# One expert tile fewer, and the last two shared tiles finished one by one on VectorE

## The reference

```
scores = softmax(xf @ gate_w.T)
weights, idx = top_k(scores, 2)
eo   = (silu(xf @ w1[e].T) * (xf @ w3[e].T)) @ w2[e].T      # for each expert e
y    = sum over the two chosen experts of weight * eo
z    = silu(xf @ ws1.T) * (xf @ ws3.T) @ ws2.T              # the shared expert
x    = layernorm(x + y + z)                                  # the block's output
```

## Time and profile before

| | |
|---|---|
| time, median of 3 runs | 1658.03 us (1657.46 to 1659.5) |
| time of the profiled execution | 1656.27 us |
| span of the profiled execution | 1654.5 us |
| PE busy | 1608.0 us, 97% of the span |
| DVE, ACT, POOL busy | 820.9, 654.7, 706.5 us |
| granted TensorE clock, mean | 0.99 |

### The profile page before, as it was taken

The page is one execution under the profiler, slowest core; times in us unless marked ns, Lnnn a source line. Parts: engine busy times, 40 slices in busy tenths (PEclk is TensorE's granted clock), DMA queues, the critical chain, the costliest instruction groups (busy, mean ns, idle before and its releaser), DMA issues.

```text
span 1654.5 us, 31031 instructions
## 1 busy us (share of the span) xinstructions
PE 1608.0 (97%) x9466; PEld 1352.2 (82%) x9467; DVE 820.9 (50%) x2239; ACT 654.7 (40%) x1564; POOL 706.5 (43%) x774
## 2 busy tenths in 40 slices
PE   7999999999999999999999999897999999999997
PEld 6898999899999989998999899875677777777764
DVE  5555556655655656566556655565222222222365
ACT  4444334433443344334334433443233333333455
POOL 3323333333343243333432433433555555555465
PEclk9899999999999999999999999999999999999999
DMA  8112111110111020111111201348355555556686
GB/s 287 35 62 60 33 33 52 44 32 32 52 43 32 32 63 32 32 32 63 32 32 32 63 32 32 115 139 270 87 102 103 102 102 103 102 104 126 198 302 234
DMA packets 83916, 143.19 MB, mean 87 GB/s; under 512 B 10664, under 2 KB 27560, under 8 KB 83328
## 3 DMA queue, kind: packets, MB, share of 16 engines
q1 hardware_dynamic: 59792, 95.96, 17.6%
q0 software_dynamic: 18304, 38.24, 13.2%
q10 hardware_dynamic: 5776, 8.43, 1.9%
HBM read 94.75 MB, written 56.76 MB: 92 GB/s over the span
## 4 chain that ended last, share of the span: by engine, by line
PE 92%; DMA 3%; DVE 2%; issue 1%; POOL 1%; ACT 1%; SPq 0%; ACTq 0%; POOLq 0%; DVEq 0%
PE bank L1151 32%; PE bank L1076 16%; PE bank L1245 11%; PE bank L1103 10%; PE bank L1226 7%; PE bank L1200 6%; PE bank L1184 3%; PE bank L1213 3%; PE bank L1050 3%; DMA bx<-x_d 1%; PE bank L1086 1%; DMA passing<-in_wqkvT 1%; DMA bx<-x_d,idxc 0%; DVE zs L1740 0%; POOL w13l L719 0%
## 5 line engine op out<-in xcount | busy, mean ns | idle before, releaser
L1151 PE MATMUL bank<-wh,xh 128*128 128x512 f32 (+2 forms) x896 | 338.8, 378 | 2.8 <-DVE wl L1355 2.8
L1151 PE MATMUL bank<-wl,xh 128*128 128x512 f32 (+2 forms) x896 | 327.5, 365 | 0.0
L1151 PE MATMUL bank<-wh,xl 128*128 128x512 f32 (+2 forms) x896 | 326.7, 365 | 0.0
L668 POOL TENSOR_TENSOR rnorm<-ssmax,nhalf 128x4 f32<-128x4 f32 x128 | 131.8, 1030 | 389.8 <-DVE ssmax L1391 384.6
L1151 PEld LDWEIGHTS bank<-wh,xh 128*128 128x128 f32 x896 | 170.1, 190 | 29.7 <-DVE wl L1355 2.2
L1151 PEld LDWEIGHTS bank<-wh,xl 128*128 128x128 f32 x896 | 169.8, 190 | 28.4
L1151 PEld LDWEIGHTS bank<-wl,xh 128*128 128x128 f32 x896 | 170.3, 190 | 22.5
L1377 DVE TENSOR_TENSOR bl<-bank,bh 128x512 fp32r<-128x512 f32 x104 | 71.6, 689 | 179.0 <-ACT bh L830 178.9
L756 POOL DMA_INDIRECT eo_d<-eo,dstc x72 | 115.3, 1602 | 101.4 <-ACT eo L1015 76.4
L1245 PE MATMUL bank<-woh,oh 128*128 128x256 f32 (+1 forms) x512 | 147.5, 288 | 0.9 <-DVE xr L1461 0.9
L1245 PE MATMUL bank<-wol,oh 128*128 128x256 f32 (+1 forms) x512 | 144.8, 283 | 0.0
(11 more groups left out here) (201 smaller groups left out, 3490.4 us busy)
## 6 DMA issues: line engine op xcount, KB each, us to landing
eo_d<-zero_d SPq DMA_DIRECT2D x34, 256.0 KB, 3.0
xt<-in_xT SPq DMA_DIRECT2D x33, 256.0 KB, 3.2
xr<-in_x SPq DMA_DIRECT2D x32, 256.0 KB, 2.7
x_d<-xr SPq DMA_DIRECT2D x32, 256.0 KB, 2.1
eo_d<-xr SPq DMA_DIRECT2D x32, 256.0 KB, 2.3
bx<-x_d SPq DMA_DIRECT2D x32, 256.0 KB, 5.7
ga<-eo_d SPq DMA_DIRECT2D x16, 512.0 KB, 5.4
gb<-eo_d SPq DMA_DIRECT2D x16, 512.0 KB, 6.9
```

Source lines behind the costliest of these rows:

```text
L668: pool.tensor_tensor(rnorm[:, :], ssmax[:, :], nhalf[:, :], ALU.pow).then_inc(rn_s, 1)
L1151: mm = pe.matmul(b[:, 0:n], a[:, par, c, :], wt[:, c, cols], start=(c == 0 and k == 0), stop=(c == DC - 1 and k == 2))
```

## The change

Three things change. First, `NX` stays 71. A few constants follow: the pattern of `jp128` is still made for an even count (`NXP` = 72), the two semaphores that count the scatters of even and odd tiles wait for 36 and 35 of them, and the written-out tail of `tile_steps` starts at step 76 in place of 80, so the hardware loop has 15 iterations in place of 16 and three more expert tiles are written out behind it.

Second, for the last pair the product of each tile is not copied into `zs` by ACT. DVE's new `finish_tile` adds the bank and `ga` of one tile (128x512) into `zs`, takes its statistics, adds eps, waits for POOL's one power instruction (`tile_power`), and subtracts the mean and multiplies with a `tensor_scalar` into `oo`. It does this for tile 30, then for tile 31. Third, SP's last two stores wait for DVE's new semaphore `last_s`.

```diff
-NX += NX % 2
+NXP = NX + -NX % 4
...
-            for q in range(S1 + NX - 4, NQ + 1):
+            for q in range(4 * ((S1 + NX - 4) // 4), NQ + 1):
...
-                    sp.wait_ge(o_s, 2 * n + k + 1)
+                    sp.wait_ge(*((last_s, k + 1) if n == LAST else (o_s, 2 * n + k + 1)))
...
-                        sp.wait_ge(exo_out[i], 16 * NX // 2)
+                        sp.wait_ge(exo_out[i], 16 * len(range(i, NX, 2)))
...
+            def tile_power(k):
+                r = rs2[:, LAST % 2, k:k + 1]
+                pool.wait_ge(fve, 2 * LAST + k + 1)
+                pool.tensor_tensor(r, r, nhalf[:, 0:1], ALU.pow).then_inc(frs, 1)
...
-                    pair_power(n)
+                    if n < LAST:
+                        pair_power(n)
+                if q0 >= NQ - 1:
+                    tile_power(q0 - NQ + 1)
...
             def combine(n):
-                if 1 <= n <= PAIRS:
+                if 1 <= n <= LAST:
                     normalise(n - 1)
...
-                if q0 - 1 >= FIRST:
+                if FIRST <= q0 - 1 < NQ - 2:
...
+            def finish_tile(k):
+
+                z, b = z_of(LAST)[:, k, :], LAST % 2
+                dve.wait_ge(gab_s, LAST + 1)
+                dve.wait_ge(eo_s, NQ - 1 + k)
+                dve.tensor_tensor(z, bank[6 + (NQ + k) % 2][:, :], ga[:, LAST % 4, k, :], ALU.add).then_inc(y_s, 1)
+                dve.wait_ge(y_s, lates(LAST) + k)
+                if k == 0:
+                    dve.wait_ge(fnm, LAST)
+                m = 2 * LAST + k
+                dve.wait_ge(fmv, m)
+                dve.bn_stats(bn6[:, :], z).then_inc(fbn, 1)
+                dve.wait_ge(fbn, m + 1)
+                dve.bn_aggr(mv2[:, b, k, :], bn6[:, :]).then_inc(fmv, 1)
+                dve.wait_ge(fmv, m + 1)
+                dve.tensor_scalar(rs2[:, b, k:k + 1], mv2[:, b, k, 1:2], EPS, None, ALU.add).then_inc(fve, 1)
+                dve.wait_ge(frs, LAST + 1 + k)
+                if k == 0:
+                    dve.wait_ge(o_out[b], 32 * (LAST // 2))
+                dve.tensor_scalar(oo[:, b, k, :], z, mv2[:, b, k, 0:1], rs2[:, b, k:k + 1], ALU.subtract, ALU.mult)\
+                   .then_inc(last_s, 1)
...
             def combine(n):
-                if n < PAIRS:
+                if n < LAST:
                     total(n)
...
+                if q0 >= NQ - 1:
+                    finish_tile(q0 - NQ + 1)
```

More of the change, by code:

```diff
@@ L196, in block_kernel @@
         jx = sbuf(sb, "jx", [P, NX, E])
-        jp128 = sbuf(sb, "jp128", [P, NX])
+        jp128 = sbuf(sb, "jp128", [P, NXP])
         idx_u = sbuf(sb, "idx_u", [P, NX], U32)
@@ L210, in block_kernel @@
         dstc = sbuf(sb, "dstc", [P, E, 1], U32)
-        sbuf(sb, "to_the_shared_low_part", [P, 3 * H * P // 2 - NX * (E + 7) - 14 * E])
+        sbuf(sb, "to_the_shared_low_part", [P, 3 * H * P // 2 - NX * E - NXP * 7 - 14 * E])
         sh13l = sbuf(sb, "sh13l", [P, DC, GRP], F32R)
@@ L315, in block_kernel @@
         y_s = sem("y_s")
+        last_s = sem("last_s")
         fbn = sem("fbn")
@@ L418, in block_kernel @@
         SLOT_Q = S1 - 3
+        LAST = PAIRS - 1
         EARLY = S1 // 2
@@ L635, in table_constants @@
                           allow_small_or_imprecise_dtypes=True).then_inc(b_const, 1)
-                pool.iota(jp128[:, :], pattern=[[0, NX // 2], [P, 2]], base=0, channel_multiplier=1,
+                pool.iota(jp128[:, :], pattern=[[0, NXP // 2], [P, 2]], base=0, channel_multiplier=1,
                           allow_small_or_imprecise_dtypes=True).then_inc(b_const, 1)
@@ L1724, in slot_contents @@
                 then(dve.scalar_tensor_tensor(out=slot_f[:, 1, :], in0=slot_f[:, 0, :], scalar=float(2 * T),
-                                              in1=jp128[:, :], op0=ALU.is_ge, op1=ALU.mult))
+                                              in1=jp128[:, 0:NX], op0=ALU.is_ge, op1=ALU.mult))
                 then(dve.tensor_tensor(slot_f[:, 1, :], slot_f[:, 0, :], slot_f[:, 1, :], ALU.add))
```

## The result

| | before | changed |
|---|---|---|
| median of 5 runs | 1657.46 us (1656.59 to 1659.5) | 1647.57 us (1645.78 to 1648.85) |
| profiled execution, its time and span | 1656.27, 1654.5 us | 1645.78, 1644.0 us |

A forecast was written before the change was run, and what follows sets the result against it. PE, busy 97% of the span, was taken to bound the kernel. The removed tile's -5.13 us and the tail's -3.2 sum to -8.3, from the median 1658.03 to 1649.7 us; range 1647.3 to 1652.3.

The forecast's parts named there:

- The removed tile, -5.13 us: Stretch of expert tiles: one tile's PE work is all on the path, -5.13 us (bounds -5.1 to -5.4).
- Three tiles written out, late shared rows, table work, 0: Behind the loop, shared-row loads and 71-column tables: each 0; bounds -0.1/+0.5, up to +2.7, and -0.1/+0.1 us.
- The tail, -3.2 us: Behind PE's last product: DVE finishes tiles 30 and 31, last store's input ready at 1648.8, -3.2 us (-3.8 to -1.5).
- The estimate by the page: Tail's last DVE operation: the skill page's estimate of 0.42 us for 512 elements, against the row's 0.54 for 520.
- What comes after the expert tiles ... moves forward as a block: Behind the expert tiles: everything is tied to them by tile counts, so it moves forward together with the -5.13 us.
- PE's wait of 1.2 us at the ninth step: Ninth step after `FIRST`: PE's wait of some 1.2 us was expected to remain in the profile after.
- the sum: Whole kernel: -5.13 for the tile and -3.2 for the tail make -8.3 us.
- Rival 1: DVE's and POOL's adds behind `FIRST` meet otherwise: 1647.9 us without the first meeting, 1651.1 if worse at 1638; chance 0.15.
- That both engines slow each other: Rival 1's reading of the adds at 1585.30 us: DVE's took 3.17 us during POOL's 2.41, alone 1.23.
- Rivals 2 to 4: Tail gives nothing, 1652.9 us (0.07 with late loads); loop pauses, 1662.2 (0.03); 72nd tile already skipped, 1654.8 (no room).

The follow-up runs named there:

- twelve traces: All traces of four kernels: 72 tiles old tail (five), 72 new tail (two), 71 old tail (two), 71 new tail (three); delay 0.00 to 1.73 us.
- the second: The unmodified changed kernel timed once more against the kernel before: ratio 0.9947 [0.9933, 0.9961], -8.8 us.

## Why the prediction was right or wrong

- *The removed tile, -5.13 us.* Right: 5.09 in the first pair of traces, 5.07 between the averages. PE had no gap before and has none now.
- *Three tiles written out, late shared rows, table work, 0.* Right for the first two: the written-out tiles are in the 344.0 to 344.7 us, and in the traces of both kernels PE has no wait in the first eight steps from `FIRST` on, so no late shared tile waited for its load. The table work lies at 1114 to 1150 us, ahead of step 16, where the variation of that stretch hides its 0.1 us.
- *The tail, -3.2 us.* Right in its steps: the wait on `fnm` was the late one (0.86 us idle), tile 31 waited for DVE and not for its product, the power took 0.55 (0.56 forecast), the last operation 0.55 (0.54). It gave 3.36. My terms, unrounded, end at 1648.76 us and give -3.26. The other 0.10 are in DVE's hand-over from tile 30 to tile 31, where from the start of the last operation on tile 30 to the add of tile 31 it took 0.46 us and I had put 0.54, and in a few hundredths elsewhere.
- *The estimate by the page.* VectorE: DVE Perf Modes (section on the perf-mode tier table) of the Trainium skill gives an estimate of 0.42 us for the last operation on 512 elements; the trace has 0.55. The row of L1515 was the better guide.
- *"What comes after the expert tiles ... moves forward as a block".* This is the step that failed, together with a term that the sum does not have at all, the stretch ahead of step 16. I took PE's wait of 1.2 us at the ninth step for a fixed part of the kernel and named it as a mark to look for; the changed kernel's first trace did not have it. Rival 1 had the meeting of the adds, with 0.15 between two sides, but it should have been in the forecast's own range: the delay is 0.00 to 1.73 us in twelve traces, and turns on which of two instructions starts first. Nor did I allow for the stretch ahead of step 16, which ends at 1190.0 to 1199.3 us in the same traces. In the first pair of traces the stretch ahead gave -1.35 us and the stretch behind `FIRST` -0.70 (-1.38 and +0.68), where the sum had 0 for both. The medians lay 2.1 us beyond the sum in the first comparison and 0.5 in the second. Both intervals hold -8.3, so the medians alone do not show an excess.
- *Rival 1, its reading and its number.* "That both engines slow each other" was read wrongly from the earlier trace rows: POOL's add took 2.41 us there, no more than alone, and only DVE's was slow. That the median, 1647.57 us, lies near the rival's 1647.9 is luck. It let the add of pair 14 get faster by 0.6 us, and that add got slower by 0.67; what filled the gap came from ahead of step 16, which the rival does not name.
- *Rivals 2 to 4.* The hand-overs between DVE and POOL stayed below 0.1 us, the loop's code cost nothing, and the tile was really computed before.
- GPSIMD Engine Reference (section Key points) of the Trainium skill names the sharing of SBUF interfaces for VectorE instructions with two SBUF inputs. The traces agree: L1750's add, with both inputs in SBUF, is slowed and the new add with one input in a bank took 0.68 to 0.69 us throughout, also at 1634.76 us, with POOL's small instructions under way.

Open is what makes the load into `gb` land earlier or later, why the first stretch varies, and whether the medians' 2.1 and 0.5 us beyond the sum are more than chance. No run here takes the other DMA traffic away.

## What to carry to other kernels

A wait read from one trace is a sample. Where two engines race for something by a few hundredths of a microsecond, its price belongs into the range with both outcomes, and a second trace of the unchanged kernel tells it more cheaply than any argument. Where PE was busy without a gap, a removed tile was worth its pace, here 5.07 to 5.09 us for 5.13; and in a tail, a counter that two chains share can be the wait that ends last, as `fnm` was here.

## What was not expected of the hardware

- Of two float32 adds of 128x1024 from SBUF, one on DVE and one on POOL, the one that starts first runs at its full speed and the other takes about as much longer as the first still has to run: DVE 1.23 and POOL 3.42 us when DVE was 0.04 us ahead, DVE 3.48 and POOL 2.40 when both began in the same hundredth. Alone they take 1.22 and 2.4. When both start together, the loser's time is close to the sum of both, 1.23 + 2.4 = 3.6. A start within 0.02 us does not tell the winner: POOL's add lost with 0.02 us ahead in the changed kernel's first trace (1623.37 us, 3.49 long) and won with as much in the second (1610.98 us).
- A small instruction can lose too: POOL's multiplication of 128x2, 0.20 us alone, took 1.26 behind DVE's add, and that cost PE 0.96 us by way of ACT.
- The changed kernel reached step 16 at 1190.0, 1191.6 and 1199.3 us in three executions, and most of the largest difference lay around the load at 1110 us, while its stretch of expert tiles varied by 0.45 us.
